# A decoder block in float32 on one core: cross attention and feed-forward put into one loop

## Chip, cores, metric

One core of a Trainium2 chip. The metric is the device time of one execution in microseconds; lower is better. The kernel before takes 930.27 us (median of 3 runs, 928.88 to 931.19).

## What is computed

x is (16, 256, 256): 16 units of 256 tokens with 256 features. Three sublayers follow each other, each behind a layer norm and with a residual:

```python
x = x + attn(layernorm(x), ...)                   # x1: linear attention over 16 heads, gelu layer
x = x + xattn(layernorm(x), ctx, ctx, ...)        # x2: softmax attention over 256 context tokens of width 128
x = x + ffn(layernorm(x), ...)
# ffn: 8 experts that share wi and wo and differ by an adapter of rank 16; the two best have count 1, the others 0
gate = count_e * (sum of the two best softmax scores)
inter = x @ wi.T + bi + (x @ lora_A[e].T) @ lora_B[e].T
out += gate * (relu(inter) @ wo.T + bo)
```

## The kernel before

Every product in the three sublayers is made from pairs of fp32r tiles, `_hi` and `_lo`: `product` (L630) issues three matmuls, hi x lo, lo x hi, hi x hi, each with 256 or 512 moving columns. A tile is split by a cast or copy into `_hi` and a subtraction into `_lo`.

The program has five stages, one after the other: weights and projections, heads, mixing (`m_`), cross attention (`c_`), feed-forward (`f_`). Each engine has its own list of steps per stage. `over_units(eng, units, [(lag, step), ...])` runs the list once for each t and calls each step with the unit t - lag; so the order of a list is the order of the instructions on that engine, and each engine works them strictly in that order, stopping at semaphores. The first steps are written out, the middle is a hardware loop of two units per turn.

```python
for lag, emit in stages:
    if pair is not None:
        emit(Unit(pair, t - lag, deepest - lag))
    elif 0 <= t - lag < units:
        emit(Unit(0, t - lag, t - lag))
```

**Cross attention**, per unit: x1 comes from DRAM (`load_x1`), VectorE takes moments (L1225, L1230), GpSimd the reciprocal root by a power of -0.5 (`rstd`, L1596 and L1598), VectorE normalises (L1236), TensorE transposes (`turn_cx`), ScalarE and VectorE split. Then `queries`, `scores`, the maximum of a row (`c_max` L1413 to L1423), `c_exps` (L1119), `turn_p`, `value`, `crossed`, and `c_residual` (L1443), which makes c_y = x2. SyncE stores x2 to DRAM (`store_x2`) and the next stage loads it again (`load_x2`).

**Feed-forward**, per unit: the same normalisation; `adapters_in` gives gate logits and the adapters' inner values; `f_shift` and `f_rank` on VectorE rank the experts in a chain of small operations and make two masks; `f_masked` multiplies the inner values with the mask of the best expert and forms the difference to the second. The 1024 hidden features are four parts j of two 128-column blocks: `hidden_first` accumulates x @ wi and the best expert's adapter in a PSUM bank, ScalarE takes relu (L1164); `hidden_second` adds the difference on top of the same bank, which gives the second expert's value, and ScalarE takes relu again; GpSimd adds the two (`f_sums`, L1677); VectorE splits the sum (`hidden_split`, L1548 and L1550); `fed(j)` multiplies with wo; `f_residual` adds. The output bias is `borow`, scaled by twice the gate (L1521).

Before the feed-forward starts, TensorE waits for all c_y (`pe.wait_ge(c_yd, 2 * UNITS)`), and before cross attention for all m_y.

## Time and profile before

| | |
|---|---|
| median of 3 runs | 930.27 us |
| the profiled execution | 931.96 us, its span 930.2 us |
| TensorE matmuls busy | 694.4 us (75%) |
| TensorE weight loads busy | 630.3 us (68%) |
| VectorE busy | 585.0 us (63%) |
| ScalarE busy | 335.6 us (36%) |
| GpSimd busy | 296.3 us (32%) |
| granted TensorE clock, mean | 0.835 |

The profile names engines PE (TensorE; PEld its weight loads), DVE (VectorE), ACT (ScalarE), POOL (GpSimd), SP (SyncE). Matmuls overlap in the records (each lasts from its issue until its result is there), so a busy PE says little about its rate; the distance of their starts does. Means over the span mix stages: the mixing stage ends at about 432 us, cross attention at 584, feed-forward at 930.

### The profile page before, as it was taken

The page shows a single profiled execution, that of the slowest core. Times are in us where ns is not written, and L with a number is a line of the kernel's source. Part 1 is how long each engine was busy: PE and PEld are TensorE (multiplying, and loading weights), DVE is VectorE, ACT ScalarE, POOL GpSimd, SP SyncE. Part 2 cuts the span into 40 slices and gives each one's busy share as a digit, 9 for nine tenths or more (in the row PEclk, how much of TensorE's full clock was granted, in tenths as well). Part 3 has the DMA queues.
Part 4 walks back from the last instruction along what each step waited for, and adds up shares of the span by engine and source line. Part 5 has one row for each costly group of instructions (what it writes and reads, how often), then busy time and mean ns, then how long its engine had stood idle before and what let it go on. Part 6 is the DMA issues. An engine that isn't in the chain of part 4 may idle for free. (4 is left out here: it accounts for less than half of the span.)

```text
span 930.2 us, 22413 instructions
## 1 busy us (share of the span) xinstructions
PE 694.4 (75%) x8314; PEld 630.3 (68%) x8314; DVE 585.0 (63%) x1467; ACT 335.6 (36%) x797; POOL 296.3 (32%) x313
## 2 busy tenths in 40 slices
PE   4785885756664467665656675499999999999997
PEld 3664764655554356565545564399999999999997
DVE  5654642222222677775888887568877888887773
ACT  4463641112112444441433333133444333434432
POOL 0222310000003988872334342023333323233322
PEclk9997985555565577777888878589999999999999
DMA  8387796455641233341222222000011000001000
GB/s 239 85 170 196 192 203 81 71 93 98 105 122 48 79 103 101 101 124 46 74 69 73 68 73 80 23 13 23 25 31 38 23 23 23 23 23 45 13 13 24
DMA packets 95271, 71.04 MB, mean 76 GB/s; under 512 B 31192, under 2 KB 91872, under 8 KB 95200
## 3 DMA queue, kind: packets, MB, share of 16 engines
q1 hardware_dynamic: 94240, 66.89, 28.4%
q10 hardware_dynamic: 960, 3.15, 1.9%
q8 instruction: 51, 0.84, 0.4%
q14 instruction: 20, 0.16, 0.1%
HBM read 40.66 MB, written 29.36 MB: 75 GB/s over the span
## 5 line engine op out<-in xcount | busy, mean ns | idle before, releaser
L1164 ACT ACTIVATE f_h<-banks,bic 128x256 f32<-128x256 f32 x256 | 102.1, 474 | 83.0 <-PE banks L630 65.9
L1677 POOL TENSOR_TENSOR f_hs<-f_h 128x512 f32<-128x512 f32 x64 | 85.6, 1349 | 135.4 <-ACT f_h L1164 131.8
L1316 DVE TENSOR_TENSOR h_sm<-banks,blockmask 128x1024 f32<-128x1024 f32 x32 | 37.7, 1219 | 114.6 <-PE banks L741 114.6
L1598 POOL TENSOR_TENSOR m_rh<-m_ms,mhalf 128x32 f32<-128x32 f32 x16 | 88.3, 5517 | 1.3
L1548 DVE CAST f_hT_hi<-f_hs 128x512 fp32r<-128x512 f32 x64 | 44.1, 689 | 62.3 <-POOL f_hs L1677 62.3
L630 PE MATMUL banks<-f_adT_hi,lbT_lo 128*128 128x256 f32 x256 | 72.8, 284 | 12.4 <-ACT f_h L1164 12.4
L630 PE MATMUL banks<-woT_hi,f_hT_lo 128*128 128x256 f32 x256 | 74.5, 291 | 1.0 <-DVE f_hT_lo L1550 1.0
L759 PE MATMUL banks<-h_sm,h_v 64*16 64x64 f32 x2048 | 36.7, 297 | 50.1 <-issue 50.1
L630 PE MATMUL banks<-f_xT_hi,wiT_lo 128*128 128x256 f32 x256 | 73.0, 285 | 0.3 <-DVE f_adT_lo L1540 0.3
L630 PE MATMUL banks<-woT_lo,f_hT_hi 128*128 128x256 f32 x256 | 71.5, 279 | 0.0
L630 PE MATMUL banks<-f_xT_lo,wiT_hi 128*128 128x256 f32 x256 | 71.5, 279 | 0.0
L630 PE MATMUL banks<-f_xT_hi,wiT_hi 128*128 128x256 f32 x256 | 71.5, 279 | 0.0
L630 PE MATMUL banks<-woT_hi,f_hT_hi 128*128 128x256 f32 x256 | 71.4, 279 | 0.0
L630 PE MATMUL banks<-f_adT_lo,lbT_hi 128*128 128x256 f32 x256 | 71.1, 278 | 0.0
L630 PE MATMUL banks<-f_adT_hi,lbT_hi 128*128 128x256 f32 x256 | 71.1, 278 | 0.0
L759 PEld LDWEIGHTS banks<-h_sm,h_v 64*16 64x16 f32 x2048 | 28.5, 119 | 56.1 <-issue 54.4
L1042 ACT ACTIVATE h_wT<-banks 128x512 f32<-128x512 f32 x32 | 17.4, 595 | 126.1 <-PE banks L759 126.1
L1596 POOL TENSOR_SCALAR m_ms<-m_ss 128x32 f32<-128x32 f32 x16 | 4.8, 301 | 176.8 <-DVE m_ss L1328 176.3
L630 PEld LDWEIGHTS banks<-f_adT_hi,lbT_lo 128*128 128x128 f32 x256 | 48.4, 189 | 15.5 <-ACT f_h L1164 15.5
L630 PEld LDWEIGHTS banks<-woT_hi,f_hT_lo 128*128 128x128 f32 x256 | 48.2, 188 | 3.5 <-DVE f_hT_lo L1550 2.8
L630 PEld LDWEIGHTS banks<-f_xT_hi,wiT_lo 128*128 128x128 f32 x256 | 49.0, 191 | 0.5 <-DVE f_adT_lo L1540 0.5
L630 PEld LDWEIGHTS banks<-f_xT_lo,wiT_hi 128*128 128x128 f32 x256 | 48.9, 191 | 0.0
(253 smaller groups left out, 2160.4 us busy)
## 6 DMA issues: line engine op xcount, KB each, us to landing
qk_scratch<-p_qk SPq DMA_DIRECT2D x32, 256.0 KB, 2.4
h_qk<-qk_scratch SPq DMA_DIRECT2D x20, 256.0 KB, 8.9
xin<-in_x_dram SPq DMA_DIRECT2D x8, 512.0 KB, 5.1
v_scratch<-p_v SPq DMA_DIRECT2D x16, 256.0 KB, 4.1
h_v<-v_scratch SPq DMA_DIRECT2D x16, 256.0 KB, 8.1
attn_scratch<-h_wn SPq DMA_DIRECT2D x16, 256.0 KB, 5.3
m_w<-attn_scratch SPq DMA_DIRECT2D x16, 256.0 KB, 2.8
m_x<-in_x_dram SPq DMA_DIRECT2D x16, 256.0 KB, 2.9
```

Source lines behind the costliest of these rows:

```text
L630: ins = pe.matmul(acc, left(a), right(b), start=first and n == 0, stop=last and n == 2, skip_group_check=skip)
L759: ins = pe.matmul(bank[4 + c][32 * i:32 * i + HD, g * HT:(g + 1) * HT], h_v[HT * c:HT * c + HT, u.slot, :, PG * i + GR * r + g], h_sm[HT * ...
L1042: act.activation(to[:, :, PG * c + GR * r:PG * c + GR * r + GR], bank[4 + c][:, :].rearrange("p (g x) -> p x g", g=GR), ACT.Copy).then_inc ...
L1164: ins = act.activation(out_slot[:, j % 2, c * T:(c + 1) * T], bank[4 + j][:, c * T:(c + 1) * T], ACT.Relu, bias=bic[:, f:f + 1])
L1316: dve.tensor_tensor(h_sm[:, r, 2 * s:2 * s + 2], pairs[s][:, :, :], blockmask[:, :].rearrange("p (o n) -> p o n", o=1).broadcast_to([P, 2, ...
L1548: dve.tensor_copy(hi, f_hs[:, j % 2]).then_inc(f_hhi, 1)
L1596: pool.tensor_scalar(tmp, src, scale, add, ALU.mult, ALU.add).then_inc(step_sem, 1)
L1598: pool.tensor_tensor(out_ap, tmp, mhalf[:, 0:width], ALU.pow).then_inc(done, 1)
L1677: pool.tensor_tensor(f_hs[:, j % 2], f_h1[:, j % 2], f_h2[:, j % 2], ALU.add).then_inc(f_hsd, 1)
```

## The change

Cross attention and feed-forward become one list per engine. A step t works cross attention of unit t - 1, normalisation and gates of unit t - 2, the hidden layer of unit t - 3 and the last products of unit t - 4. x2 stays on chip: `f_moments`, `f_normalise` and `f_gate` read c_y; `store_x2`, `load_x2` and the DRAM scratch go. Further:

- relu(z + b) of the second expert is written max(z, -b) + b, so that one VectorE instruction (`total`) takes the maximum and adds the first expert's relu. The b that is missing then is put into the output bias: row 2 bo + bi @ wo, made once before the mixing stage by 16 float32 matmuls on TensorE (L756 of the changed kernel), copied by ScalarE (`brow`), added by VectorE. `f_vs2` is no longer needed.
- The `_hi` of the hidden tile and of the adapter tile is made on ScalarE (`high`, `f_adhigh`) instead of VectorE, the `_lo` of the hidden tile on GpSimd (`remainder`) instead of VectorE.
- The normalisations go to ScalarE (`normalised`: x * rstd + (-mean * rstd)), for which GpSimd makes -mean * rstd (`scales`).
- The row constant of the scores is a product on GpSimd and a sum on VectorE (`c_constant`) instead of one VectorE instruction with an accumulator; the bias bv is added to c_x in place.
- The hidden layer has three PSUM banks in rotation instead of four, and all cross attention tiles but c_x, c_c and c_y have one buffer instead of two.

```diff
--- before.py
+++ after.py
-        x2_d = nc.dram_tensor("x2_scratch", (UNITS, T, D), F32).ap()
...
+            def start_tail():
+                first_two(load_x1)
+                first_two(load_context)
                 sp.dma_start(borow[:, :], bo.rearrange("(a n) -> a n", a=1).broadcast_to([P, D])).then_inc(s_w["rows"], 16)
...
+            over_units(sp, UNITS, [(0, but_first_two(load_context)), (0, but_first_two(load_x1)), (4, store_out)])
...
+            spread = m_y[:, :, :, :].rearrange("p a i (b n) -> p (a i b) n", n=P)
+            pe.wait_ge(s_bwide, 1)
+            for f in range(FT):
+                for part in range(2):
+                    ins = pe.matmul(bank[7][:, 0:D], spread[:, f, :], woT[part][:, f, :].bitcast(F32),
+                                    start=f == 0 and part == 0, stop=f == FT - 1 and part == 1)
+            ins.then_inc(s_brow, 1)
...
-            over_units(pe, UNITS, [(2, turn_context), (2, queries), (3, turn_p), (2, scores), (3, value),
-                                   (1, turn_cx), (3, crossed)])
...
-            over_units(pe, UNITS, [(3, turn_masks), (2, turn_f), (4, fed(0)), (4, fed(1)), (4, fed(2)), (2, adapters_in),
-                                   (4, fed(3)), (2, turn_logits), (3, hidden_a), (3, hidden_b)])
+            over_units(pe, UNITS, [(4, fed(2)), (1, turn_cx), (3, first(0)), (4, fed(3)), (2, turn_f), (1, turn_context),
+                                   (1, queries), (3, first(1)), (2, adapters_in), (1, scores), (3, second(0)), (3, first(2)),
+                                   (2, turn_logits), (3, second(1)), (3, fed(0)), (1, turn_p), (3, first(3)),
+                                   (2, turn_masks), (1, value), (3, second(2)), (3, fed(1)), (1, crossed), (3, second(3))])
...
+            act.wait_ge(s_brow, 1)
+            act.activation(brow[:, :], bank[7][:, 0:D], ACT.Copy).then_inc(s_browd, 1)
...
+            def normalised(u, nmrd, mean_rstd, rstd, src, dst, done):
+                act.wait_ge(nmrd, nth(u, 1, 1))
+                for i in range(TT):
+                    ins = act.activation(dst[:, i], src[:, i], ACT.Identity, bias=mean_rstd[:, i:i + 1], scale=rstd[:, i:i + 1])
+                ins.then_inc(done, 1)
...
+            def high(j):
+                def emit(u):
+                    act.wait_ge(f_hsd, nth(u, 4, j + 1))
+                    if u.has(1):
+                        act.wait_ge(f_fed, nth(u, 4, j - 3))
+                    elif j == 0:
+                        act.wait_ge(m_yd, UNITS)
+                    act.activation(flat(f_hT[0][:, 2 * j:2 * j + 2, :]), f_hs[:, j % 2], ACT.Copy).then_inc(f_hhi, 1)
...
-            over_units(act, UNITS, [(2, f_split), (2, f_adapters), (2, f_exps), (3, relus_a), (3, relus_b)])
+            over_units(act, UNITS, [(4, high(3)), (1, c_split), (3, relu(0)), (2, f_normalise), (2, f_split), (1, c_context),
+                                    (1, c_queries), (3, relu(1)), (2, f_adapters), (1, c_exps), (3, high(0)), (3, relu(2)),
+                                    (2, f_exps), (3, high(1)), (1, c_psplit), (3, relu(3)), (2, f_adhigh), (1, c_osplit),
+                                    (3, high(2)), (0, c_normalise)])
...
+            def c_constant(u):
+                dve.wait_ge(c_rrd, nth(u, 1, 1))
+                dve.tensor_reduce(c_r[:, :], c_rr[:, :, :], AX_X, ALU.add).then_inc(c_rd, 1)
...
+            def total(j):
+                def emit(u):
+                    dve.wait_ge(f_more, nth(u, 4, j + 1))
+                    dve.wait_ge(f_h1d, nth(u, 4, j + 1))
+                    if j >= 2 or u.has(1):
+                        dve.wait_ge(f_hlo, nth(u, 4, j - 1))
+                    for c in range(2):
+                        f = 2 * j + c
+                        ins = dve.scalar_tensor_tensor(out=f_hs[:, j % 2, c * T:(c + 1) * T], in0=bank[4 + j % 3][:, c * T:(c + 1) * T],
+                                                       scalar=nbic[:, f:f + 1], in1=f_h1[:, j % 2, c * T:(c + 1) * T],
+                                                       op0=ALU.max, op1=ALU.add)
+                    ins.then_inc(f_hsd, 1)
...
+            dve.wait_ge(s_browd, 1)
+            dve.scalar_tensor_tensor(out=borow[:, :], in0=borow[:, :], scalar=2.0, in1=brow[:, :],
+                                     op0=ALU.mult, op1=ALU.add).then_inc(s_borow, 1)
+            dve.wait_ge(s_borow, 1)
+            dve.tensor_scalar(nbic[:, :], bic[:, :], -1.0, None, ALU.mult).then_inc(s_nbic, 1)
+            dve.wait_ge(s_nbic, 1)
+            over_units(dve, UNITS, [(4, total(3)), (2, c_residual), (2, f_moments), (1, c_low), (2, f_low), (1, c_clow), (1, c_usplit),
+                                    (4, f_residual), (1, c_constant), (1, c_max), (3, total(0)), (2, f_shift), (3, total(1)), (2, f_rank),
+                                    (1, c_plow), (2, f_gate), (2, f_masked), (1, c_olow), (2, f_adlow), (3, total(2)), (0, c_moments)])
...
-                ins = dve.tensor_reduce(f_vs[:, u.slot], f_top[:, :, :], AX_X, ALU.add)
-                ins.then_inc(f_vsd, 1)
...
+            def scales(u, step_sem, var, mv, tmp, rs, nm, rstd_done, mean_done):
+                rstd(u, step_sem, (var, nth(u, 1, 1)), mv[:, :, 1], 1.0, LN_EPS, tmp, rs, TT, rstd_done)
+                pool.wait_ge(rstd_done, nth(u, 1, 1))
+                apart(pool)
+                for i in range(TT):
+                    ins = pool.tensor_scalar(nm[:, i:i + 1], mv[:, i, 0:1], rs[:, i:i + 1], -1.0, ALU.mult, ALU.mult)
+                ins.then_inc(mean_done, 1)
...
+            def remainder(j):
+                def emit(u):
+                    pool.wait_ge(f_hhi, nth(u, 4, j + 1))
+                    if u.has(1):
+                        pool.wait_ge(f_fed, nth(u, 4, j - 3))
+                    elif j == 0:
+                        pool.wait_ge(m_yd, UNITS)
+                    hi, lo = (flat(f_hT[p][:, 2 * j:2 * j + 2, :]) for p in range(2))
+                    pool.tensor_tensor(lo, f_hs[:, j % 2], hi.bitcast(F32), ALU.subtract).then_inc(f_hlo, 1)
...
-            over_units(pool, UNITS, [(1, f_rstds), (3, f_sums(0)), (3, f_sums(1)), (3, f_sums(2)), (3, f_sums(3))])
+            over_units(pool, UNITS, [(4, remainder(3)), (2, f_rstds), (1, c_constant), (1, c_natural), (1, c_with_bias),
+                                     (3, remainder(0)), (3, remainder(1)), (3, remainder(2)), (0, c_rstds)])
```

ScalarE, at the end of one step and the start of the next (`f_hT_hi` is `high`, `c_xn` is `c_normalise`, `f_h` a relu). Before, in the feed-forward:

```order
L1141 ACTIVATE f_xT_hi<-banks 128x512
L1147 ACTIVATE f_lT<-banks 128x256
L1150 ACTIVATE f_a<-banks 128x256
L1156 ACTIVATE f_ex<-f_sh 128x16
L1164 ACTIVATE f_h<-banks,bic 128x256 x16
```

In the changed kernel:

```order
L1135 ACTIVATE f_adT_hi<-f_ad 128x512
L1103 ACTIVATE c_oT_hi<-banks 128x256
L1156 ACTIVATE f_hT_hi<-f_hs 128x512
L1057 ACTIVATE c_xn<-c_x,c_nm,c_rs 128x256 x2
L1156 ACTIVATE f_hT_hi<-f_hs 128x512
L1082 ACTIVATE c_xT_hi<-banks 128x512
L1144 ACTIVATE f_h<-banks,bic 128x256 x2
L1057 ACTIVATE f_xn<-c_y,f_nm,f_rs 128x256 x2
L1115 ACTIVATE f_xT_hi<-banks 128x512
```

The 16 relus of a unit have become 8, and between them stand casts and normalisations of other units: c_xn of the next unit behind high(2), and high(3) behind c_xn.

VectorE, from the ranking to the hidden tile (`f_m` the masks, `f_hs` the sum of the two relus). Before:

```order
L1501 TENSOR_REDUCE f_rk<-f_gt 128x16
L1507 TENSOR_SCALAR f_m<-f_rk 128x128 x4
L1511 SCALAR_TENSOR_TENSOR f_top<-f_rk,f_sc 128x16
L1513 TENSOR_REDUCE f_vs<-f_top 128x2
L1516 TENSOR_SCALAR f_vs<-f_vs 128x2
L1521 SCALAR_TENSOR_TENSOR f_xb<-borow,f_vs,f_x 128x256 x2
L1548 CAST f_hT_hi<-f_hs 128x512
L1550 TENSOR_TENSOR f_hT_lo<-f_hs,f_hT_hi 128x512
```

In the changed kernel:

```order
L1479 TENSOR_SCALAR f_m<-f_rk 128x128 x4
L1406 RECIPROCAL c_inv<-c_sum 128x2
L1216 TENSOR_TENSOR c_pT_lo<-banks,c_pT_hi 128x512
L1485 SCALAR_TENSOR_TENSOR f_top<-f_rk,f_sc 128x16
L1490 TENSOR_REDUCE f_vs<-f_top 128x2
L1495 SCALAR_TENSOR_TENSOR f_xb<-borow,f_vs,c_y 128x256 x2
L1506 TENSOR_TENSOR f_ad<-f_a,banks 128x256 x2
L1508 TENSOR_TENSOR f_ad<-f_ad 128x256
L1216 TENSOR_TENSOR c_oT_lo<-banks,c_oT_hi 128x256
L1513 TENSOR_TENSOR f_adT_lo<-f_ad,f_adT_hi 128x512
L1523 SCALAR_TENSOR_TENSOR f_hs<-banks,nbic,f_h 128x256 x2
L1205 BN_STATS c_st<-c_x 128x6 x2
```

Two steps of cross attention (c_pT_lo, c_oT_lo) stand between the gates' steps, and the sum of part 2 (f_hs) and the next unit's moments (c_st) behind all of them.

## Rows read from the trace of the kernel before

**Rows 1.** Busy time by stretch: us, PE, PEld, DVE, ACT, POOL; clock, DMA share, GB/s

```profile
452.00:584.00 132.00, 82.64 (x493) 71.16 (x491) 110.03 (x296) 48.73 (x129) 49.26 (x82) 0.87 0.24 72
...
748.00:788.00 40.00, 38.26 (x331) 37.49 (x331) 31.76 (x92) 15.58 (x40) 12.62 (x12) 1.00 0.09 26
```

**Rows 2.** Tiles c_y and f_y: ns min/median/max, first and last start us

```profile
L1443 DVE SCALAR_TENSOR_TENSOR c_y<-banks,c_inv,c_xb x32: 474/480/484, 452.6 to 583.6; 128x256 f32<-128x256 f32 x32
...
L1566 DVE SCALAR_TENSOR_TENSOR f_y<-banks,f_vk,f_xb x32: 473/478/487, 627.7 to 927.0; 128x256 f32<-128x256 f32 x32
```

**Rows 3.** Timeline of PE in feed-forward: start us, us, what [idle before]

```profile
759.16 0.38 PE L630 MATMUL banks<-f_adT_hi,lbT_lo 128*128 128x256 f32 x1 [0.87 <-ACT f_h L1164]
759.38 0.29 PE L630 MATMUL banks<-f_adT_lo,lbT_hi 128*128 128x256 f32 x1
...
759.63 0.28 PE L630 MATMUL banks<-f_adT_hi,lbT_lo 128*128 128x256 f32 x1
759.74 0.28 PE L630 MATMUL banks<-f_adT_lo,lbT_hi 128*128 128x256 f32 x1
...
760.21 0.61 PE L683 MATMUL banks<-identf,f_xn 128*128 128x128 f32 x4
```

**Rows 4.** Timelines of DVE and ACT in cross attention, from the maximum to the exponentials

```profile
503.87 0.68 DVE L1413 TENSOR_REDUCE c_mx<-banks 128x2 f32<-128x512 f32 x1
...
504.95 0.22 DVE L1423 SCALAR_TENSOR_TENSOR c_nb<-c_r,bqbk,c_mr 128x2 f32<-128x2 f32 x1
...
505.20 0.47 ACT L1119 ACTIVATE c_p<-banks,c_nb 128x256 f32<-128x256 f32 x1 [1.11 <-DVE c_nb L1423]
...
506.02 0.20 ACT L1119 ACTIVATION_READ_ACCUMULATOR c_p<-banks,c_nb 128x1 f32 x1
```

**Rows 5.** Groups by line: busy us, mean ns of one | idle before

```profile
L1164 ACT ACTIVATE f_h<-banks,bic 128x256 f32<-128x256 f32 x256 | 102.1, 474 | 83.0 <-PE banks L630 65.9 <-POOL f_hs L1677 16.0
...
L1090 ACT ACTIVATE m_hT_hi<-m_g 128x512 fp32r<-128x512 f32 x16 | 10.1, 630 | 0.9
```

**Rows 6.** Timeline of DVE in feed-forward: the ranking and the masked values

```profile
750.54 0.16 DVE L1483 TENSOR_REDUCE f_sm<-f_ex 128x2 f32<-128x16 f32 x1
...
752.86 0.64 DVE L1507 TENSOR_SCALAR f_m<-f_rk 128x128 bf16<-128x128 f32 x4
753.41 0.17 DVE L1511 SCALAR_TENSOR_TENSOR f_top<-f_rk,f_sc 128x16 f32<-128x16 f32 x1
...
765.09 0.74 DVE L1531 TENSOR_TENSOR f_ad<-f_a,banks 128x256 f32<-128x256 f32 x2
765.87 0.43 DVE L1533 TENSOR_TENSOR f_ad<-f_ad 128x256 f32<-128x256 f32 x1
```

**Rows 7.** Timelines of POOL and DVE at the same time

```profile
754.00 1.29 POOL L1677 TENSOR_TENSOR f_hs<-f_h 128x512 f32<-128x512 f32 x1 [4.32 <-ACT f_h L1164]
...
754.13 1.84 DVE L1521 SCALAR_TENSOR_TENSOR f_xb<-borow,f_vs,f_x 128x256 f32<-128x256 f32 x2
```

**Rows 8.** Tile f_hs: its instructions, ns min/median/max, first and last start

```profile
L1677 POOL TENSOR_TENSOR f_hs<-f_h x64: 1272/1288/1598, 613.4 to 921.1; 128x512 f32<-128x512 f32 x64
...
L1550 DVE TENSOR_TENSOR f_hT_lo<-f_hs,f_hT_hi x64: 691/693/693, 615.2 to 923.8; 128x512 fp32r<-128x512 f32 x64
```

**Rows 9.** Timeline of POOL in cross attention: the reciprocal root

```profile
508.87 0.19 POOL L1596 TENSOR_SCALAR c_ve<-c_mv 128x2 f32<-128x2 f32 x1 [5.21 <-DVE c_mv L1230]
509.14 0.71 POOL L1598 TENSOR_TENSOR c_rs<-c_ve,mhalf 128x2 f32<-128x2 f32 x1
```

**Rows 10.** Timelines of ACT at the start of mixing, of PE in setup

```profile
293.27 0.62 ACT L1066 ACTIVATE m_sq<-m_w 128x512 f32<-128x512 f32 x1
...
24.95 1.03 PE L669 MATMUL banks<-xqT,bkwide 128*128 128x256 f32 x4
25.82 0.50 PE L671 MATMUL banks<-bqc,bkwide 128*128 128x1 f32 x4
```

**Rows 11.** Busy time by stretch in cross attention, columns as in rows 1

```profile
510.00:520.00 10.00, 6.46 (x40) 5.79 (x39) 8.34 (x23) 3.42 (x9) 3.94 (x7) 0.83 0.25 76
```

More of the change, by code:

```diff
@@ L182, in decoder @@
         PROJECT = 17400
-        CROSS = MIX - (48 * 256 + 112)
         def below(name, words, where):
@@ new lines, in second @@
+            def second(j):
+                def emit(u):
+                    pe.wait_ge(f_h1d, nth(u, 4, j + 1))
+                    for c in range(2):
+                        ins = product(pe, bank[4 + j % 3][:, c * T:(c + 1) * T],
+                                      lambda p: lbT[p][:, (2 * j + c) * P:(2 * j + c + 1) * P],
+                                      lambda p: f_adT[u.slot][p][:, 1, :], False, True, True)
+                    ins.then_inc(f_more, 1)
+                return emit
@@ L1154, in f_exps @@
                 if u.has(1):
-                    act.wait_ge(f_xbd, nth(u, 1, 0))
+                    act.wait_ge(f_vsd, nth(u, 1, 0))
                 act.activation(flat(f_ex[:, :, :]), flat(f_sh[:, :, :]), ACT.Exp).then_inc(f_exd, 1)
-            def relus(u, j, ready, out_slot, done, back):
-                act.wait_ge(ready, nth(u, 4, j + 1))
-                if j >= 2 or u.has(1):
-                    act.wait_ge(f_hsd, nth(u, 4, j - 1))
-                for c in range(2):
-                    f = 2 * j + c
-                    ins = act.activation(out_slot[:, j % 2, c * T:(c + 1) * T], bank[4 + j][:, c * T:(c + 1) * T],
-                                         ACT.Relu, bias=bic[:, f:f + 1])
-                ins.then_inc(done, 1)
@@ new lines, in relu @@
+            def relu(j):
+                def emit(u):
+                    act.wait_ge(f_base, nth(u, 4, j + 1))
+                    if j >= 2 or u.has(1):
+                        act.wait_ge(f_hsd, nth(u, 4, j - 1))
+                    for c in range(2):
+                        f = 2 * j + c
+                        ins = act.activation(f_h1[:, j % 2, c * T:(c + 1) * T], bank[4 + j % 3][:, c * T:(c + 1) * T],
+                                             ACT.Relu, bias=bic[:, f:f + 1])
+                    ins.then_inc(f_h1d, 1)
+                return emit
@@ L1321, in _ @@
             over_units(dve, SU, [(1, head_masked(r)) for r in range(ROUNDS)])
+            for i in range(2):
+                dve.wait_ge(p_stored[i], 96 * (SU // 2))
+            spread = m_y[:, :, :, :].rearrange("p a i (b n) -> p (a i b) n", n=P)
+            dve.wait_ge(s_w["rows"], 16 * N_ROWS)
+            for f in range(FT):
+                ins = dve.tensor_scalar(spread[:, f, :], identf[:, :], 0.0, bic[:, f:f + 1], ALU.mult, ALU.add)
+            ins.then_inc(s_bwide, 1)
             def m_sums(u):
```

483 lines of the change are left out of this document (198 added, 285 removed).

## The prediction

> **What bounds the kernel now.** I read the stretches by stage first, then the tiles that end each unit, then the timelines of one unit. Cross attention (432 to 584 us) ends a unit every 8.7 us: the first pair of c_y starts at 452.6 and the last one 15 units later at 583.2, 0.4 before the last single c_y [rows 2]. There the engines pass one unit from hand to hand: TensorE is busy 83 of 132 us, VectorE 110 [rows 1]. The feed-forward (584 to 930) ends one every 19.9 us: f_y from 627.7 to 926.6 [rows 2]. Here TensorE is the bound: in a 40 us stretch its weight loads alone are busy 37.5 us at a granted clock of 1.00 [rows 1], and its one wait per unit is 0.87 us for a relu [rows 3]. So a unit costs 8.7 + 19.9 = 28.6 us in steady state; the two pipelines fill in 20.5 us (432.1 to 452.6) and 44.5 us (583.2 to 627.7), and the end takes 3.6. Together 130.6 + 299 + 68.6 = 498.2 us, from 432 to 930.2. What can be won is the fill, and TensorE's idle time in cross attention.
>
> **What TensorE needs per unit after.** Matmuls of 256 columns start 0.113 us apart (759.63 to 759.74; over a unit 0.114), the second after a wait 0.22 behind the first, and a matmul's result is there 0.28 after its start, so 0.17 after the next could start; four transposes last 0.61 to their result, and the next group can start after 0.36 [rows 3]. The 156 of the feed-forward and 24 of cross attention are 20.5 us, 16 transposes and mask products about 1.5, some 23 openings 2.3: 24.3 us. If nothing else bound the loop, that would be the period.
>
> **What the order makes of it.** Every engine works its list in order, so I walked one step, durations from rows, 0 being the end of c_normalise, the last entry of ScalarE's step. A result passes to another engine in 0.03 to 0.06 us (c_nb ends at 505.17, c_p starts at 505.20, [rows 4]).
> - TensorE: turn_cx 0.36, first(0) with 18 matmuls 2.2; relu(0) 0.84 [rows 3, 5] ends at 3.7; f_normalise stands behind it on ScalarE, two ACTIVATEs like the relus, 0.84: 4.5. It waited for nothing else: fed(3) is done at 4.1.
> - TensorE: turn_f 0.36, turn_context 0.13, queries 0.8, first(1) 2.1, adapters_in 1.5, scores 0.8: 10.25. c_max on VectorE takes 1.3 from the reduce to the end of c_nb [rows 4]: 11.75. c_exps takes 1.02 [rows 4] and total(0), behind c_max, two like f_y, 0.88 [rows 2]; high(0) stands behind c_exps and takes 0.63, as m_hT_hi does [rows 5]: 13.3. remainder(0) on GpSimd, 1.29 like f_hs [rows 8], ends at 14.65.
> - TensorE meanwhile: second(0), first(2), turn_logits, second(1): 14.1. f_shift 0.5, total(1) 0.88, then f_rank, 2.9 from f_sm to the last f_m [rows 6].
> - **The price of the remainders on GpSimd.** When a POOL f_hs held the SBUF, the VectorE instruction with two SBUF inputs that came second, f_xb, took 1.84 for two instead of 0.88 [rows 7]; and an f_hs that came during VectorE's f_hT_lo took up to 1598 ns instead of 1288 [rows 8]. f_sh and eight of f_rank's instructions have two SBUF inputs, and remainder(0) and (1) fall on them. f_sh waits until 14.7, remainder(1) (16.35 to 17.65) takes f_rank out for 1.2: it ends at 19.65 instead of 18.0. Bounds: 0 (f_hT_lo, a TENSOR_TENSOR too, never took over 693 ns, though it never came second, [rows 8]) and 2.6 (two full remainders). I take 1.5 net, nearest to the f_xb row. The Trainium skill, "SBUF — State Buffer", § Who interferes with whom, says the same of all VectorE instructions with two SBUF inputs against GpSimd reads, whoever is second being blocked for the whole instruction; by it the small ones wait too and the sum stands, while by f_hT_lo's row alone it would be some 22 us less.
> - VectorE then: c_plow 0.7 (TENSOR_TENSORs of 512 take 0.69, [rows 8]), f_gate 0.41 + 0.88, f_masked 1.2 [rows 6, 7]: 22.8. ScalarE f_adhigh 0.63, c_osplit 0.38; VectorE c_olow 0.4, f_adlow 0.65, total(2) 0.87; ScalarE high(2) 0.63; GpSimd remainder(2) 1.3: 27.7. Behind it stand c_rstds: 0.19 + 0.71 [rows 9] and two more small ones, with gaps 1.5: 29.2. c_normalise 0.84: **30.1 us per step**, 5.8 more than TensorE needs and 1.5 more than the two stages need now. TensorE waits before fed(2) (second(3) ended long ago), before turn_cx, before fed(0) or turn_masks, and before crossed.
>
> **Fill and end.** Step 0, from the end of mixing: c_moments, c_rstds, c_normalise, 3.8 us. Step 1 is cross attention of unit 0 alone, with TensorE at half clock: its part 7.4 (turn_cx 1.1, turn_p 1.1, queries, scores and value 1.75 each), splits, c_max and c_exps 7.0, and 3.7 for the next unit's c_moments to c_normalise, which stand behind c_olow: 18.1. Step 2 adds the gates of unit 0: 8.1 to the end of adapters_in, 4.4 for scores, c_max, c_exps and f_exps, f_rank 2.9, c_plow 0.7, f_gate 1.3, f_masked 1.2, then 2.0 to f_adlow and 3.6 to c_normalise: 24.2. Together 46. Then 13 steps (3 to 15) of 30.1 = 391.3, 3 more for the first of them on a cold clock; step 16 ends with fed(2) at 27.7 + 1.5 = 29.2; step 17 has no cross attention, but the same circle from second(1) over f_rank and f_masked to fed(2): 24.9; step 18 only hidden layers: 18.4; fed(3) of the last unit, residual and store 6.1 (the last f_y to the end is 3.6 now). Sum 518.9, against 498.2: **+20.7**.
>
> **The row of the output bias.** 16 float32 matmuls of 256 columns before the mixing stage. TensorE starts them when ScalarE has written the last h_wn, and ScalarE waits for them before its first m_sq, which now starts without any idle time behind that h_wn, at 293.27 [rows 10]. L669 shows that such a matmul is two records, two of them 0.87 us, 0.43 each [rows 10]: 6.9, plus copy and hand-overs 0.6. Nothing behind m_sq has slack: all of mixing hangs on it. **+7.5** (at half clock 14; TensorE transposes without a break just before, so I take the fast end).
>
> **What costs nothing.** x2 no longer goes out and back: SyncE issues 32 transfers fewer and the waits of load_x1 on c_yd end 20 us before c_moments needs the tile; nothing waited for f_x before, so nothing is gained (if x1's 2.7 us were late, c_moments would wait). VectorE's own work is about 20 us of 30, ScalarE's 14, GpSimd's 13: none is a bound; if f_rank or c_exps grew, total(2) would be late by as much. The casts on ScalarE (0.63 for 0.43) and total in place of two steps are in the walk.
>
> **Sum.** +20.7 + 7.5 = +28.2 on the profiled execution (span 930.2, time 931.96). The median of the three runs is 930.27, 1.7 below it; the difference applies to it: **958 us**.
>
> **Rivals.**
> - *GpSimd does not hold VectorE's small instructions.* The period is 28.6, as now; 15 steps less 1.5: 958 - 22 = 936. For it f_hT_lo's 693 ns. 0.17.
> - *The clock falls.* TensorE idles a fifth of each step, in the feed-forward it had none of this and ran at 1.00; cross attention, idle for over a third, ran at 0.83 in ten-us stretches such as 510 to 520 [rows 11], which means a third of the time at 1.2 GHz. 12.1 us of the chain are TensorE's; with half of that share, 16%, it lengthens by 1.9 a step: 14 x 1.9 = 27, 985 us. The Trainium skill, "TensorE: Matmul & The Clock Gate", § A second HAM failure mode, says that frequent short idle times between groups let the clock swing. Against it: no gap in the walk is over 2 us. 0.15.
> - *TensorE stays the bound, with every tile there in time (faster).* The place is turn_cx: if the normalised tile is there when fed(2) ends, the circle never closes and the period is 24.3. Steps 3 to 16 give 5.8 less each, 81, the last two 3: 874. For it: each engine alone has slack. It decides where the walk of 30.1 is too long by a fifth; I found no link that can be skipped, since c_rstds stands behind remainder(2) by position. 0.10.
> - *The walk counts each link somewhat too long (faster, less).* Period 27.2: 14 x 2.9 = 41 less, 917. 0.13.
> - *The change doesn't do what it says.* The order shows it does; not priced.
>
> **The numbers.** The forecast case has 0.45, its own range is 946 to 970 (bounds of the port price and of the bias row). 0.3% of this kernel is 2.8 us, about what a measurement can tell. Faster takes the two faster rivals, 0.23; between the walk without the port price and the faster walk there is 0.05 for no change; slower 0.72. The range leaves out the TensorE-bound case and the worse end of the clock: 915 to 985.
>
> **What would show it.** Right: c_y pairs 30 us apart; m_sq first at about 300.8; TensorE waiting in each step for c_xn and for f_hT_lo; a wait of turn_f for f_xn; f_gt or f_eq with maxima over 1 us; granted clock near 1.00. Wrong: c_y pairs 24 to 27 us apart; TensorE without waits over 0.5 us; the first m_sq unmoved; or a clock under 0.9 in the loop, which would bring the time over 970.

## The result, and the profile after

The changed kernel takes 970.91 us (median of 4 runs, 969.93 to 972.24), the kernel before, beside it on the same chip, 929.58 (926.44 to 931.19): a ratio of 1.045, 95% interval 1.0419 to 1.0481. It is slower by 41 us. The forecast was 958 with a range of 915 to 985. The profiled execution spans 969.2 us, against 930.2.

The tiles that carried the prediction, of the changed kernel (ns min/median/max, first and last start in us), to be held against [rows 2, 8, 10]:

```profile
L1025 ACT ACTIVATE m_sq<-m_w x16: 621/630/636, 299.8 to 411.7; 128x512 f32<-128x512 f32 x16
L1205 DVE BATCH_NORM_STATS2 c_st<-c_x x32: 406/413/427, 438.0 to 884.4; 128x6 f32<-128x256 f32 x32
L1057 ACT ACTIVATE c_xn<-c_x,c_nm,c_rs x32: 584/592/600, 441.1 to 888.7; 128x256 f32<-128x256 f32 x32
L1420 DVE SCALAR_TENSOR_TENSOR c_y<-banks,c_inv,c_x x32: 472/474/484, 458.4 to 916.2; 128x256 f32<-128x256 f32 x32
L1449 DVE TENSOR_TENSOR f_sh<-f_lg,f_mx x16: 174/991/1007, 471.1 to 930.0; 128x16 f32<-128x16 f32 x16
L1468 DVE TENSOR_TENSOR f_eq<-f_eq,tril x32: 209/221/1200, 473.2 to 933.6; 128x64 f32<-128x64 f32 x32
```

Mixing starts at 299.8 instead of 293.3, the merged loop (first c_st) at 438.0 instead of 432.1: 5.9 us of the loss are made before the loop. From there to the end it is 531.2 us instead of 498.1: 33 in the loop. The pairs of c_y are (916.2 - 0.4 - 458.4) / 15 = 30.5 us apart. The c_xn of one step starts 30.8 us after that of the step before in all steps from the sixth on, but for one with 33.1.

Where TensorE waits in one such step (timeline of PE of the changed kernel, only rows with idle time before them; in brackets how long and for whom):

```profile
701.46 0.38 PE L599 MATMUL banks<-woT_hi,f_hT_lo 128*128 128x256 f32 x1 [1.79 <-POOL f_hT_lo L1659]
704.52 0.65 PE L652 MATMUL banks<-identf,c_xn 128*128 128x128 f32 x4 [1.38 <-ACT c_xn L1057]
709.38 0.65 PE L652 MATMUL banks<-identf,f_xn 128*128 128x128 f32 x4 [0.69 <-ACT f_xn L1057]
719.75 0.38 PE L599 MATMUL banks<-woT_hi,f_hT_lo 128*128 128x256 f32 x1 [0.85 <-POOL f_hT_lo L1659]
724.32 0.40 PE L871 MATMUL banks<-identb,f_m 128*128 128x128 bf16 x4 [0.34 <-DVE f_m L1479]
724.97 0.38 PE L599 MATMUL banks<-c_pT_hi,c_ch_lo 128*128 128x256 f32 x1 [0.26 <-DVE c_pT_lo L1216]
728.90 0.39 PE L599 MATMUL banks<-xwv_hi,c_oT_lo 128*128 128x256 f32 x1 [0.84 <-DVE c_oT_lo L1216]
732.38 0.39 PE L599 MATMUL banks<-woT_hi,f_hT_lo 128*128 128x256 f32 x1 [1.78 <-POOL f_hT_lo L1659]
```

In order these are fed(2), turn_cx, turn_f, fed(0), turn_masks, value, crossed, and fed(2) of the next step: 6.1 us of waits in 30.9. Before, the feed-forward had 0.87 per unit [rows 3]. Each wait is for an instruction that stands behind others in the list of its engine; which of them costs, the experiments tell.

### The profile page after: what moved, and what is told of

It is laid out like the page before. It is cut to its first block, busy times and chain, and to the rows that moved or that the text cites. A ratio compares the mean times of both kernels' runs of the same rounds, so it can differ in the third digit from the quotient of the medians.

```text
span 969.2 us, 22130 instructions
## 1 busy us (share of the span) xinstructions
PE 703.3 (73%) x8346; PEld 635.1 (66%) x8346; DVE 516.9 (53%) x1317; ACT 367.3 (38%) x814; POOL 327.2 (34%) x393
## 3 DMA queue, kind: packets, MB, share of 16 engines
q1 hardware_dynamic: 85536, 58.50, 24.4%
## 4 chain that ended last, share of the span: by engine, by line
PE 38%; issue 25%; DVE 20%; POOL 7%; ACT 7%; DMA 2%; SPq 1%; DVEq 1%; POOLq 0%; ACTq 0%
PE banks L599 21%; PE banks L710 4%; PE banks L728 4%; PE banks L743 3%; DVE f_hs L1523 2%; PE banks L652 2%; POOL f_hT_lo L1659 2%; ACT f_xn L1057 2%; DMA xin<-in_x_dram 1%; DVE m_t L1328 1%; POOL c_rs L1570 1%; DVE m_at L1321 1%; ACT c_xn L1057 1%; DVE f_ad L1506 1%; DVE m_n L1315 1%
## 5 line engine op out<-in xcount | busy, mean ns | idle before, releaser
L1659 POOL TENSOR_TENSOR f_hT_lo<-f_hs,f_hT_hi 128x512 fp32r<-128x512 f32 x64 | 82.9, 1296 | 293.7 <-ACT f_hT_hi L1156 291.9
L1144 ACT ACTIVATE f_h<-banks,bic 128x256 f32<-128x256 f32 x128 | 53.5, 469 | 90.2 <-PE banks L599 90.1
L599 PE MATMUL banks<-f_xT_hi,wiT_lo 128*128 128x256 f32 x256 | 76.4, 298 | 0.0
L599 PE MATMUL banks<-f_xT_lo,wiT_hi 128*128 128x256 f32 x256 | 73.6, 288 | 0.0
L599 PE MATMUL banks<-f_xT_hi,wiT_hi 128*128 128x256 f32 x256 | 73.6, 287 | 0.0
L728 PEld LDWEIGHTS banks<-h_sm,h_v 64*16 64x16 f32 x2048 | 28.8, 119 | 53.5 <-issue 51.7
L1523 DVE SCALAR_TENSOR_TENSOR f_hs<-banks,nbic,f_h 128x256 f32<-128x256 f32 x128 | 55.6, 476 | 15.0 <-PE banks L599 11.4
L1156 ACT ACTIVATE f_hT_hi<-f_hs 128x512 fp32r<-128x512 f32 x64 | 40.2, 628 | 42.9 <-DVE f_hs L1523 42.9
```

The costliest lines, as they stand in the source:

```text
L599: ins = pe.matmul(acc, left(a), right(b), start=first and n == 0, stop=last and n == 2, skip_group_check=skip)
L728: ins = pe.matmul(bank[4 + c][32 * i:32 * i + HD, g * HT:(g + 1) * HT], h_v[HT * c:HT * c + HT, u.slot, :, PG * i + GR * r + g], h_sm[HT * ...
L1144: ins = act.activation(f_h1[:, j % 2, c * T:(c + 1) * T], bank[4 + j % 3][:, c * T:(c + 1) * T], ACT.Relu, bias=bic[:, f:f + 1])
L1156: act.activation(flat(f_hT[0][:, 2 * j:2 * j + 2, :]), f_hs[:, j % 2], ACT.Copy).then_inc(f_hhi, 1)
L1523: ins = dve.scalar_tensor_tensor(out=f_hs[:, j % 2, c * T:(c + 1) * T], in0=bank[4 + j % 3][:, c * T:(c + 1) * T], scalar=nbic[:, f:f + 1] ...
L1659: pool.tensor_tensor(lo, f_hs[:, j % 2], hi.bitcast(F32), ALU.subtract).then_inc(f_hlo, 1)
```

## Experiments

Four single changes to the changed kernel came first.

### e1: the bias row's copy behind mixing

```diff
-            act.wait_ge(s_brow, 1)
-            act.activation(brow[:, :], bank[7][:, 0:D], ACT.Copy).then_inc(s_browd, 1)
             over_units(act, UNITS, [(4, m_gelus), (3, m_split), (2, m_squares3), (0, m_squares)])
+            act.wait_ge(s_brow, 1)
+            act.activation(brow[:, :], bank[7][:, 0:D], ACT.Copy).then_inc(s_browd, 1)
```

> ScalarE's copy of the bias row moves from ahead of the mixing stage to behind it; the 16 float32 matmuls stay where they are on TensorE. Theory (the step of the prediction on the bias row): ScalarE's first m_sq no longer waits for TensorE, it goes back from 299.8 to about 293.3, and the start of the merged loop (first c_st, 438.0) follows, by 5.9, which is what the trace of the changed kernel shows of it at that point. TensorE's first turn of the mixing stage comes some 12 us after the first m_sq, so that the 6.9 us of matmuls are hidden. Time 970.9 - 6 = 965. Rival: the matmuls delay TensorE's first turn, or ScalarE's copy at the end delays the first c_xn: 1 to 3 us gained only.

962.16 us (ratio 1.0342, 1.0299 to 1.0384): 8.7 less. Its first m_sq:

```profile
L1022 ACT ACTIVATE m_sq<-m_w x16: 621/632/634, 290.7 to 401.5; 128x512 f32<-128x512 f32 x16
```

Expected were 965 and a first m_sq at about 293.3. One trace would say that the wait cost 9.1 us. But the earlier stages do not end at the same time in every execution: with ScalarE's wait five kernels have their first m_sq from 296.4 to 299.8, 298.5 on average, without it eight of these experiments have it from 290.2 to 295.7, 293.1 on average. So the wait costs about 5.4 us; the rest of the 8.7 is within what the two 95% intervals leave open. The copy behind mixing costs nothing that shows: the first c_st comes 137.5 us after the first m_sq, in the changed kernel 138.2. All later versions with new lists keep this.

### e2: c_moments and c_rstds earlier

```diff
 dve:  ... (2, f_masked), (1, c_olow), (2, f_adlow), (3, total(2)), (0, c_moments)
    -> ... (2, f_masked), (0, c_moments), (1, c_olow), (2, f_adlow), (3, total(2))
 pool: ... (3, remainder(2)), (0, c_rstds)  ->  ... (0, c_rstds), (3, remainder(2))
```

> Two moves in the merged loop: VectorE does c_moments before c_olow instead of behind total(2), GpSimd does c_rstds before remainder(2) instead of behind it. Nothing else changes. Theory (the circle of the prediction: total(2), high(2), remainder(2), c_rstds, c_normalise, turn_cx): c_xn is then there when fed(2) ends, so that turn_cx follows fed(2) at once. A step loses c_rstds with its gaps (1.8) and c_normalise (1.1), less fed(2) itself (1.4), which is then on the path: 1.5 us less per step, period 29.3 instead of 30.8, time 971 - 15 x 1.5 = 948. Rival 1: the circle was not what set the period, since TensorE also waits 0.7 to 1.8 us at four other places in the step; they grow by what is gained: under 5 us gained. Rival 2: the early c_moments and c_rstds push back c_olow, total(2) and remainder(2), which stand behind them, by up to 1 us: 960 or more.

958.18 us (1.0300, 1.0263 to 1.0337): 12.7 less, not 22. TensorE's wait for c_xn is gone, and c_y pairs came 28.7 to 29.4 us apart while the clock was at 1.00, 1.6 less than before, as expected. But from 620 us on they came 30.7 to 31.0 apart. Busy time by stretch says why (columns as in [rows 1]); this is the kernel of e2 in one of those steps:

```profile
706.00:716.00 10.00, 8.41 (x71) 7.85 (x70) 8.57 (x30) 3.92 (x10) 2.56 (x2) 1.00 0.00 0
716.00:722.00 6.00, 3.35 (x26) 2.94 (x26) 5.36 (x15) 3.04 (x6) 3.63 (x6) 0.99 0.00 0
722.00:725.40 3.40, 3.40 (x18) 3.40 (x18) 0.43 (x3) 0.60 (x1) 3.02 (x6) 0.51 0.26 77
725.40:736.00 10.60, 9.95 (x86) 9.75 (x85) 4.21 (x9) 4.63 (x11) 2.76 (x5) 1.00 0.11 37
```

Behind 6 us in which TensorE was busy 3.4, the granted clock fell to 0.5 (1.2 GHz) for 3.4 us: work of 1.7 us at the full clock, so 1.7 lost per step. The changed kernel has such a fall too, but only once in the steady part, and longer:

```profile
602.00:608.00 6.00, 3.38 (x27) 2.97 (x26) 4.95 (x14) 1.45 (x3) 2.16 (x3) 1.00 0.00 0
608.00:615.00 7.00, 5.83 (x30) 5.57 (x29) 1.09 (x4) 2.43 (x5) 4.79 (x9) 0.52 0.13 37
```

It is the step that took 33.1. But a stretch so empty does not by itself bring the clock down. The changed kernel has one like it in every step, at a clock of 1.00, here two of them:

```profile
698.00:704.00 6.00, 3.35 (x24) 2.95 (x24) 4.88 (x15) 1.33 (x3) 2.66 (x5) 1.00 0.00 0
729.00:735.00 6.00, 3.28 (x24) 2.87 (x24) 4.79 (x15) 1.49 (x3) 2.67 (x5) 1.00 0.06 18
```

So what tells the steps with a fall from those without stays open. The gain on the path was real, 1.6 us per step, and about half of it came through; the rest went back as clock. The Trainium skill, "TensorE: Matmul & The Clock Gate", § A second HAM failure mode, which the prediction cited, has frequent short idle times making the clock swing; e2's steps agree, the changed kernel's, nearly all at 1.00, do not.

### e3: both normalisations back on VectorE

```diff
+            def normalised(u, rstd_done, mv, rs, src, dst, done):
+                dve.wait_ge(rstd_done, nth(u, 1, 1))
+                for i in range(TT):
+                    ins = dve.tensor_scalar(dst[:, i], src[:, i], mv[:, i, 0:1], rs[:, i:i + 1], ALU.subtract, ALU.mult)
+                ins.then_inc(done, 1)
-                    ins = pool.tensor_scalar(nm[:, i:i + 1], mv[:, i, 0:1], rs[:, i:i + 1], -1.0, ALU.mult, ALU.mult)
```

> Both normalisations go back to VectorE, as one two-operation instruction per half on mean and factor (in its list behind c_residual and behind c_low), and GpSimd's products of mean and factor (c_nm, f_nm) fall away. Theory (that moving them to ScalarE put links on the circle): c_nm (0.50 and a gap of 0.25) goes, and two ACTIVATEs (1.09) become two VectorE instructions of about 0.4 each, 0.75 together: 1.1 us less before turn_cx and, with relu(0) no longer in front, 1.1 less before turn_f, whose wait for f_xn is only 0.7. Together 1.8 us less per step, 29.0; time 971 - 15 x 1.8 = 944. Rival: VectorE, busy 20 us of 30, has the instructions in the way of f_moments and f_low, and nothing is gained or up to 10 us is lost.

958.21 us (953.09 to 962.88; ratio 1.0318, 1.0270 to 1.0366): 12.7 less. Expected were 944. At the full clock the c_y pairs are 29.6 to 30.0 apart, 0.9 less; here too stretches of 0.89 and 0.94 appear, with steps of 31.7 and 32.2. TensorE's waits in one step of e3, the same view as above:

```profile
565.79 0.65 PE L652 MATMUL banks<-identf,c_xn 128*128 128x128 f32 x4 [1.19 <-DVE c_xn L1357]
580.24 0.38 PE L599 MATMUL banks<-woT_hi,f_hT_lo 128*128 128x256 f32 x1 [0.86 <-POOL f_hT_lo L1654]
```

The wait for f_xn has vanished, 0.7 as expected. The one for c_xn only fell from 1.38 to 1.19, where 1.1 less was expected. The list is not the reason: c_xn starts 0.13 us after the end of c_rs. But GpSimd begins remainder(3), which stands right behind c_rstds, just before it:

```profile
563.23 0.71 POOL L1570 TENSOR_TENSOR c_rs<-c_ve,mhalf 128x2 f32<-128x2 f32 x1
563.91 1.28 POOL L1654 TENSOR_TENSOR f_hT_lo<-f_hs,f_hT_hi 128x512 fp32r<-128x512 f32 x1
```

```profile
564.07 1.59 DVE L1357 TENSOR_SCALAR c_xn<-c_x,c_mv,c_rs 128x256 f32<-128x256 f32 x2 [0.30 <-POOL c_rs L1570]
```

The pair of c_xn takes 1.59 us instead of 0.74; its first instruction ends with GpSimd's. It is so in all 13 steps from the fourth on (1.58 to 1.63), while in the first three, with no remainder beside it, the pair takes 0.73 to 0.74. A hold by GpSimd took what the shorter instructions should have given.

### e4 and e12: what the remainders hold

```diff
 e4:
-                    pool.tensor_tensor(lo, f_hs[:, j % 2], hi.bitcast(F32), ALU.subtract).then_inc(f_hlo, 1)
+                    n = 8 if j < 2 else 512
+                    pool.tensor_tensor(lo[:, 0:n], f_hs[:, j % 2, 0:n], hi[:, 0:n].bitcast(F32), ALU.subtract).then_inc(f_hlo, 1)
 e12, for j < 2:
+                    for n in (0, 8):
+                        pool.tensor_tensor(lo[:, n:n + 8], f_hs[:, j % 2, n:n + 8], hi[:, n:n + 8].bitcast(F32), ALU.subtract)
+                    pool.tensor_tensor(f_wait[:, j], f_ve[:, :], mhalf[:, 0:TT], ALU.pow).then_inc(f_hlo, 1)
```

> remainder(0) and remainder(1) on GpSimd work on 8 of their 512 columns, the rest of the tile holds zeros (so most of the low part of half of the hidden values is left out). It takes away what holds VectorE's f_sh and f_rank, and 1.1 us of each remainder's own latency. Theory of the prediction (the held instructions are on the path, 1.5 us per step, between 0 and 2.6): f_sh falls from 991 to about 175 ns, the maxima of f_gt and f_eq over 1 us vanish, and the period falls by 1.5, time 971 - 15 x 1.5 = 948; with the wait of fed(0) for remainder(0), 0.85, gone as well up to 35 less. Rival: what VectorE gains before f_masked TensorE does not take up, since turn_masks and value wait only 0.3 each; then no more than fed(0)'s 0.85 and these 0.6 can be had, and less if crossed and fed(2) wait longer: 5 to 15 us less.

> The changed kernel, in which remainder(0) and remainder(1) are two subtractions on 8 columns each and one power on 2 columns (c_rs, such a power, takes 0.71 us), so that they take GpSimd about as long as before (1.2 us against 1.28) but read hardly anything; the rest of the tile holds zeros, most of the low part of half of the hidden values is left out. It separates two things that e4_small_remainders (954.3, 16.6 below the changed kernel) took away together: the hold on VectorE's instructions and the remainders' own latency, on which fed(0) waits. Theory of the prediction (the hold is what costs, 1.5 us per step): f_sh falls to about 0.2 us and the time is 971 - 20 = 951, like e4. Rival 1 (the hold costs half, fed(0)'s wait the other half): 962. Rival 2: GpSimd holds VectorE in a power of 2 columns just as well, f_sh stays near 0.7 us or above: over 965, and nothing is separated.

e4 took 954.33 us (1.0258, 1.0219 to 1.0297), e12 958.32 (1.0330, 1.0296 to 1.0364); expected were 948 and 951. The tiles of e12:

```profile
L1450 DVE TENSOR_TENSOR f_sh<-f_lg,f_mx x16: 174/211/220, 474.6 to 918.2; 128x16 f32<-128x16 f32 x16
L1469 DVE TENSOR_TENSOR f_eq<-f_eq,tril x32: 216/224/268, 476.7 to 920.8; 128x64 f32<-128x64 f32 x32
L1668 POOL TENSOR_TENSOR f_wait<-f_ve,mhalf x32: 693/702/708, 503.5 to 942.9; 128x2 f32<-128x2 f32 x32
```

The holds are gone (f_sh 211 ns for 991). A power on 2 columns, 0.70 us long, holds nothing to speak of: at 712.80 f_sh starts together with one and takes 0.21 us. c_y pairs at the full clock: the changed kernel 30.4, 31.0, 30.3 early and 30.3 and 31.3 in turn later, 30.7 on average; e12 29.0, 29.7, 28.8, 29.8, on average 29.3; e4 29.0, 29.6, 28.7, 29.8, also 29.3. **The hold costs 1.4 us per step; the remainders' own 1.1 us cost nothing.** This is read from the steps at the full clock, of one trace each. The totals alone do not show it, and e12's lies between its theory (951) and its rival 1 (962): from 620 to 920 us e12 has a clock of 0.89 or 0.94 in seven of ten stretches of 30 us, e4 in five, the changed kernel in none.

### e5, e6, e7: other lists

With each link worth 1 to 1.6 us, the question was how far the order of the lists alone goes. e5 makes five moves, e6 rearranges all four lists, e7 as well, with the normalisations on VectorE.

```diff
 e5, dve:  (3, total(2)) before (1, c_olow); (2, f_gate) last; (0, c_moments) behind (2, f_moments)
     pe:   (2, turn_f) behind (1, queries)
     pool: (0, c_rstds) before (3, remainder(2))
```

> The bias row as in the first experiment, and five moves in the lists of the merged loop, nothing else: VectorE does total(2) before c_olow, f_gate at the end of its list, c_moments behind f_moments; TensorE does turn_f behind queries; GpSimd does c_rstds before remainder(2). Each takes an instruction that TensorE waits for out from behind one that nobody waits for. In the step of the changed kernel that begins at 704.5 TensorE waits 1.8 us for remainder(2), 1.4 for c_xn, 0.7 for f_xn. Theory (the circle is made of positions in the lists, not of the work): these three go nearly, 3.9 us less; what then ends last are fed(0), turn_masks, value and crossed, 2.3 us together now. Period about 27, time 962 - 15 x 3.8 = 905. Rival 1: the waits move to the next place in the list, as when only c_moments and c_rstds were moved, which brought 1.5 us per step at the full clock: 940. Rival 2: TensorE's granted clock falls once per step, as it did from 620 us on in that run (0.94 instead of 1.00, steps of 30.9 instead of 29.0), and eats 2 us of each step: 935.

> The bias row as in the first experiment, and the four lists of the merged loop reordered throughout: on TensorE fed(0) and fed(1) come at the end of the step, scores behind adapters_in, turn_f behind queries, second(2) and second(3) around turn_masks; ScalarE does f_normalise before relu(0) and c_normalise in the middle of the step; VectorE does total(2) before f_masked, c_moments behind f_moments, f_gate late; GpSimd does c_rstds early. The same instructions, waits and banks. Theory (TensorE's need of 24.3 us per step is the bound once nothing is late): period 24.3 to 25, time 962 - 15 x 6.2 = 870. Rival 1: some link still ends late and 26.5 is left: 900. Rival 2: the clock falls in each step, 2 us more: 900 as well, but with 0.94 granted and no waits over 0.5 us.

> As the run before with the lists reordered throughout, but with both normalisations on VectorE, whose list has them behind f_moments. Theory (with every link off the path it no longer matters which engine does the normalisations): the same time as the run with them on ScalarE, 870. Rival: VectorE, which was busy 22.8 of 30 us with the normalisations, is then busy 22.8 of 24.5 and becomes the bound; a period of 25 to 26, 880 to 895.

e5 took 908.31 us (0.9736, 0.9709 to 0.9763; expected 905), e6 917.44 (0.9828, 0.9803 to 0.9853), e7 869.56 (0.9340, 0.9302 to 0.9378). **Five moves, with the bias row's copy behind mixing, turn 4.5% slower into 2.6% faster than before.** e5's steps are 27.3, with the clock at 1.00 in nearly all of them. e7 took the 870 that were expected, with the clock at 1.00 throughout, but its steps of 25.4 are those of its rival (25 to 26). e6, meant to be as fast as e7, missed by 47 us, with steps of 27.3 at first and 28 to 29 later, at 0.94. The wait that nobody had in e7 (waits of e6 from 560 to 800 us: total, times, longest):

```profile
DVE c_st L1202 <- DMA c_x<-x_scratch: 17.3, 9, 2.4
...
PE banks L871 <- DVE f_m L1476: 18.3, 8, 2.3
PE banks L599 <- DVE c_xT_lo L1213: 12.0, 9, 2.0
```

c_moments behind f_moments asks for c_x 1.9 us before the transfer lands, which SyncE can only start when c_residual, right ahead of it, has freed the tile. VectorE stands still for it, c_xT_lo and f_rank with it.

This wait alone does not make the difference, though: e5, 9 us faster, has it too (17.0 us in 9 waits in the same window). A difference that the traces show is in f_gate, which in e6 falls under two of GpSimd's wide instructions, one after the other. The pair of f_xb is 2.60 us long in e6, 1.50 in e5, 0.88 in the changed kernel; first e6, then e5:

```profile
701.95 2.60 DVE L1492 SCALAR_TENSOR_TENSOR f_xb<-borow,f_vs,c_y 128x256 f32<-128x256 f32 x2 [0.16 <-DVE f_vs L1487]
```

```profile
721.97 1.50 DVE L1492 SCALAR_TENSOR_TENSOR f_xb<-borow,f_vs,c_y 128x256 f32<-128x256 f32 x2
```

In e6 GpSimd is in remainder(2) and c_constant from 701.54 to 704.26. No run takes this hold away by itself.

### e8 to e11: one move each, and the last lists

> The kernel of e7_lists_vector with one move: GpSimd does c_with_bias (c_x plus a bias row, two instructions of 0.7 us) behind c_constant, at about 703.6 in a step that begins at 700, and no longer behind remainder(0), at 713.1. Theory (an instruction of VectorE with two inputs in SBUF that begins while GpSimd is in one ends with GpSimd's): in the step of e7 from 700 us on, f_eq (L1465) takes 1.34 for two instead of 0.44 because c_with_bias began at 713.12; this 0.9 goes, f_m comes 0.9 earlier, and TensorE's wait for it (0.83 before turn_masks) nearly vanishes: 0.8 less per step, 869.6 - 12 = 858. Rival: nothing comes of it, since c_with_bias then meets VectorE's copies behind turn_cx and turn_f, or since TensorE's 0.4 for f_hs grows by what is gained: 866 to 870.

> The kernel of e6_lists_scalar with one move: VectorE does c_moments behind f_low, no longer behind f_moments. Theory: in e6 VectorE waited 1.9 us in each step at c_moments for the transfer of c_x, which SyncE can only start when c_residual of two units before has freed the tile (9 waits, 17.3 us in 240 us), and everything behind it in the list, f_rank above all, was late: TensorE waited 2.3 us per step for f_m. With the move the transfer is there in time: 1.9 less per step, 917.4 - 15 x 1.9 = 889. Rival 1: the granted clock, 0.94 in most stretches of that run, does not come back, and VectorE's gain ends in other waits: over 905. Rival 2: with the waits gone TensorE is dense enough that the clock stays at 1.00 too, 3 us per step in all: 870.

> The kernel of e7_lists_vector with its lists rearranged once more, so that fewer of VectorE's instructions with two inputs in SBUF meet a busy GpSimd: c_natural, c_constant and c_with_bias stand together at the start of GpSimd's list, f_rank and c_plow before total(1) on VectorE, first(3) before second(1) on TensorE. Theory: TensorE's 1.4 us of waits per step go, the period is TensorE's 24.1 to 24.4: 869.6 - 15 x 1.1 = 853. Rival: VectorE, busy 22.8 us of 25.4 there, has no slack for its waits of some 0.05 us at each hand-over, and the time stays within 865 to 872.

> The kernel of e6_lists_scalar with its lists rearranged in the same way as e10, c_moments behind c_low, c_natural and c_with_bias behind c_rstds on GpSimd, both normalisations still on ScalarE. Theory (the engine that normalises does not matter once the links are off the path): within 1% of e10, about 855. Rival: c_moments behind c_low still waits for the transfer of c_x, some 1 us per step, and the clock falls as in e6: 880 to 900.

**e8** (e7 with c_with_bias ahead of remainder(0)): 857.74 us (0.9201, 0.9146 to 0.9255), 858 was expected. The tile f_eq, first of e7, then of e8:

```profile
L1465 DVE TENSOR_TENSOR f_eq<-f_eq,tril x32: 219/759/1204, 463.9 to 837.3; 128x64 f32<-128x64 f32 x32
```

```profile
L1465 DVE TENSOR_TENSOR f_eq<-f_eq,tril x32: 211/222/1203, 467.0 to 826.5; 128x64 f32<-128x64 f32 x32
```

Between 700 and 726 us the pair takes 1.34 us in e7 and 0.36 in e8. That is 1.0 less, and the step goes from 25.4 to 24.4. TensorE has almost nothing left to wait for (waits of PE in e8, 560 to 800 us, all of them, and its busy time, columns as in [rows 1]):

```profile
PE banks L599 <- DVE f_hs L1520: 1.9, 5, 0.4
PE banks L599 <- POOL f_hT_lo L1651: 1.6, 5, 0.3
PE banks L652 <- DVE f_xn L1354: 1.1, 7, 0.2
```

```profile
520.00:560.00 40.00, 39.67 (x335) 38.75 (x335) 34.42 (x102) 17.59 (x45) 17.61 (x22) 1.00 0.11 34
680.00:720.00 40.00, 39.10 (x329) 37.97 (x328) 35.57 (x104) 16.77 (x41) 18.58 (x22) 1.00 0.07 23
```

**e9** (e6 with c_moments behind f_low): 903.47 us (0.9695, 0.9638 to 0.9753), 14 less, half of the 28 expected. The wait for c_x is gone and the clock is back at 1.00 nearly throughout, but at the full clock the steps are 26.7 and later 27.3, where e6 had 27.2 to 27.4 early; by this most of the 14 us is the clock. TensorE's wait for f_m got longer, not shorter:

```profile
DVE f_xT_lo L1213 <- ACT f_xT_hi L1113: 16.3, 9, 1.8
DVE f_xb L1530 <- PE banks L599: 12.0, 9, 1.4
...
PE banks L871 <- DVE f_m L1476: 25.8, 9, 2.9
```

VectorE now waits at the next two entries of its list, f_residual and f_low, for what is late there. Of rival 1 of its expectation the other waits came true, but not the clock, which did come back. The hold on f_xb is still there (2.6 to 2.8 us the pair). **e10** (e7's lists rearranged): 869.70 us (0.9327, 0.9271 to 0.9382), no gain where 853 was expected: its rival (865 to 872) came true, though for another reason. TensorE waits 0.9 us per step for f_xn and 0.4 for f_hs. f_xn is late because GpSimd, in c_constant and c_with_bias from 702.09 to 704.84, holds its pair for 2.03 us instead of 0.74:

```profile
702.23 2.03 DVE L1354 TENSOR_SCALAR f_xn<-c_y,f_mv,f_rs 128x256 f32<-128x256 f32 x2 [0.67 <-POOL f_rs L1567]
```

**e11** (the same aim with the normalisations on ScalarE): 858.63 us (0.9202, 0.9145 to 0.9259; expected 855), steps of 24.2. It still waits 1.3 us per step for c_x at c_moments, but TensorE's waits for VectorE's f_m and c_pT_lo come to only 0.6 a step, so that what stands behind c_moments costs TensorE little.

e8 and e11 beat both kernels, by 8.0% the one before. Beside the bias row and e3, e8 differs from the changed kernel in its lists alone (TensorE, ScalarE, VectorE, GpSimd):

```python
over_units(pe, UNITS, [(4, fed(2)), (3, first(0)), (4, fed(3)), (1, turn_context), (1, turn_cx), (2, turn_f), (3, first(1)), (1, queries),
                       (2, adapters_in), (1, scores), (3, second(0)), (2, turn_logits), (3, first(2)), (3, second(1)), (3, first(3)), (1, turn_p),
                       (3, second(2)), (2, turn_masks), (3, fed(0)), (1, value), (3, second(3)), (3, fed(1)), (1, crossed)])
over_units(act, UNITS, [(4, high(3)), (1, c_split), (1, c_context), (2, f_split), (1, c_queries), (3, relu(0)), (2, f_adapters), (3, relu(1)),
                        (2, f_exps), (1, c_exps), (3, high(0)), (3, relu(2)), (1, c_psplit), (3, high(1)), (3, relu(3)), (3, high(2)),
                        (1, c_osplit), (2, f_adhigh)])
over_units(dve, UNITS, [(4, total(3)), (2, c_residual), (2, f_moments), (1, c_normalise), (2, f_normalise), (4, f_residual), (1, c_low), (1, c_clow),
                        (2, f_low), (0, c_moments), (1, c_usplit), (1, c_constant), (1, c_max), (2, f_shift), (3, total(0)), (2, f_rank),
                        (3, total(1)), (1, c_plow), (3, total(2)), (2, f_masked), (1, c_olow), (2, f_gate), (2, f_adlow)])
over_units(pool, UNITS, [(4, remainder(3)), (2, f_rstds), (1, c_natural), (1, c_constant), (1, c_with_bias), (3, remainder(0)),
                         (3, remainder(1)), (0, c_rstds), (3, remainder(2))])
```

Not tried: the relu sum undone by itself, and the two stages kept apart with x2 on chip.

## Why the prediction was right, and where it was off

- **The walk of the step.** Forecast 30.1 us, measured 30.8. From the end of c_normalise (704.38) f_normalise ends after 4.9 (4.5 forecast), f_rank after 19.9 (19.65), f_masked after 23.1 (22.8), remainder(2) after 27.95 (27.7), c_rstds after 29.7 (29.2), c_normalise after 30.85 (30.1). The chain is the one that was forecast; 0.5 of the 0.7 missing are two terms: c_normalise and f_normalise were put at 0.84, "two ACTIVATEs like the relus", and take 1.09 (592 ns each against 467), 0.25 each. The rest is c_rstds, 1.8 with its gaps for 1.5. The middle of the walk was somewhat short too: remainder(0) ends at 15.2 (14.65), 0.6 late, of which f_rank gave 0.4 back.
- **The price of the remainders.** Forecast 1.5 net between 0 and 2.6; e4 and e12 give 1.4. f_sh took 991 ns and waited as described.
- **TensorE's need** of 24.3: e8 and e11 run at 24.4 and 24.2, when nothing is late.
- **Fill and end.** Steps 0 to 2: 4.2 + 18.6 + 23.2 = 46.0, forecast 46. Step 3: 33.9 (33.1). Steps 4 to 15: 371.3, forecast 12 x 30.1 = 361.2; of the 10 us between them 7 lie in eleven of the steps, 0.65 each, and 3 in the one with the clock dip. Step 16 to the end: 80.0 (78.6). In all +33 instead of +20.7; that is where nearly all of the 13 us between forecast and result lie.
- **The bias row.** Forecast +7.5; the change's trace has 5.9, the average over kernels 5.4, the medians of e1 and the changed kernel 8.7. The mechanism is shown by e1.
- **Nothing else costs.** No wait for c_x is among VectorE's in the changed kernel. In e5 and e6, which ask for it earlier, it came, 1.9 us per step: "if x1's 2.7 us were late, c_moments would wait".
- **Rivals.** "GpSimd does not hold VectorE's small instructions" fell with f_sh. "The clock falls" happened for one step of the steady part, and from 620 us on in nearly every step of e2, which had less idle time (no wait for c_xn) and no longer wait than the changed kernel. It was argued from the sum of the idle time, and this does not tell the two apart; nor does the emptiest stretch of a step (see e2). So that the clock held in the forecast case was in part luck: the rival's reasoning gives no reason why it should hold there and fall in e2. "TensorE stays the bound" got 0.10 since "I found no link that can be skipped, since c_rstds stands behind remainder(2) by position". That was right for this change. It is also the cause of the slowdown: position, which costs nothing to alter.
